# Decoder kernel: the 64-tap causal filter as one 64x64 triangular block for each channel, the two short filters on GpSimd, and new orders of the steps

## The reference, cut to what matters

```
def _dwconv(x, w):                      # x: sequence, token, channel; w: channel, K taps
    K = w.shape[1]
    xt = pad(transpose(x, (0, 2, 1)), K - 1 zeros ahead)
    y = conv(xt, w[:, None, :], groups = channels)     # y[c, t] = sum_s w[c, K-1-s] * v[c, t-s]
    return transpose(y, (0, 2, 1))

v = silu(_dwconv(hs @ Wv, conv_v))
paths = stack([_dwconv(v, fir_s),       # 3 taps
               _dwconv(v, fir_m),       # 15 taps
               _dwconv(v, fir_l),       # 64 taps
               delta_path,              # delta rule, chunks of 32 tokens
               v])
gate_in = concatenate([hs, stats(paths)])          # mean, square, absolute value, norm
probs = softmax((gelu(gate_in @ gW1 + gb1) @ gW2 + gb2) / tau)
o = einsum('blhp,blhpd->blhd', probs, paths)       # then a norm and @ Wo
```

## Time and profile before

| what | value |
|---|---|
| median of 3 runs | 1418.63 us (1417.29 to 1436.04) |
| span of the profiled execution | 1418.5 us |
| PE busy in the span | 1334.8 us, 94% |
| DVE, ACT, POOL busy | 991.1, 682.2, 137.9 us (70%, 48%, 10%) |
| mean granted TensorE clock | 0.975 of full |

### The profile page before, as it was taken

How to read it: one execution, slowest core, us unless ns; L and a number is a source line. 1 busy time by engine, 2 the same in 40 slices (tenths; PEclk the granted TensorE clock), 3 DMA queues, 4 the chain that set the end, 5 groups by cost and what they waited for, 6 DMA issues and landing times.

```text
span 1418.5 us, 42978 instructions
## 1 busy us (share of the span) xinstructions
PE 1334.8 (94%) x18644; PEld 1166.4 (82%) x18644; DVE 991.1 (70%) x2959; ACT 682.2 (48%) x1735; POOL 137.9 (10%) x299
## 2 busy tenths in 40 slices
PE   6999998999986899999999999999999999999997
PEld 6788887888643689899789889788979879989976
DVE  7957898678689554667784567796457778455767
ACT  3535763448377456333447533346632444743332
POOL 3111121111110010100110100011010010010000
PEclk9989999999997899999999999999999999999999
DMA  5000000000230200000000000000000000000001
GB/s 160 2 3 2 3 2 2 3 2 3 77 139 19 77 2 1 2 3 2 2 2 1 2 3 3 1 2 1 1 2 4 2 3 1 1 1 3 3 2 31
DMA packets 8509, 20.33 MB, mean 14 GB/s; under 512 B 2304, under 2 KB 6400, under 8 KB 7808
## 3 DMA queue, kind: packets, MB, share of 16 engines
q1 hardware_dynamic: 8320, 17.58, 3.5%
HBM read 16.53 MB, written 1.05 MB: 12 GB/s over the span
## 4 chain that ended last, share of the span: by engine, by line
PE 47%; DVE 12%; ACT 4%; issue 2%; POOL 1%; DVEq 0%
PE PS L2210 6%; PE PS L2337 6%; PE PS L1935 4%; PE PS L1967 3%; PE PS L1956 3%; PE PS L1922 3%; PE PS L2220 3%; PE PS L589 2%; PE PS L690 2%; ACT AR L1985 2%; PE PS L1947 2%; PE PS L2669 1%; PE PS L2678 1%; PE PS L1819 1%; DVE X L2740 1%
## 5 line engine op out<-in xcount | busy, mean ns | idle before, releaser
L589 PE MATMUL PS<-CC 128*128 128x128 f32 x1024 | 134.9, 279 | 0.0
L589 PEld LDWEIGHTS PS<-CC 128*128 128x128 f32 x1024 | 124.5, 193 | 3.1 <-issue 0.5
L1985 ACT ACTIVATE AR<-PS,SC 128x128 f32<-128x128 f32 x256 | 91.1, 378 | 39.3 <-DVE SC L2013 39.3
L2337 PE MATMUL PS<-AR,PA 64*64 64x256 f32 (+43 forms) x2624 | 108.6, 300 | 0.5 <-issue 0.4
L2210 PEld LDWEIGHTS PS<-AR 64*64 64x64 f32 x3072 | 100.5, 135 | 7.2 <-issue 2.2
L2210 PE MATMUL PS<-AR 64*64 64x32 f32 (+1 forms) x3072 | 103.1, 219 | 0.8 <-DVE AR L2463 0.3
L576 POOL TENSOR_SCALAR SC<-mv 128x2 f32<-128x2 f32 x64 | 13.2, 206 | 837.0 <-DVE mv L562 818.4
L2337 PEld LDWEIGHTS PS<-AR,PA 64*64 64x64 f32 x2624 | 85.0, 133 | 6.9 <-issue 2.7
L2010 DVE TENSOR_REDUCE SC<-PS 128x4 f32<-128x512 f32 x64 | 44.2, 691 | 57.1 <-PE PS L1935 56.7
L1935 PE MATMUL PS<-kvt,AR 128*128 128x128 f32 x512 | 68.8, 279 | 2.6 <-ACT AR L1980 2.6
L1935 PEld LDWEIGHTS PS<-kvt,AR 128*128 128x128 f32 x512 | 63.2, 191 | 7.9 <-ACT AR L1980 6.6
(11 more groups left out here) (552 smaller groups left out, 3334.6 us busy)
## 6 DMA issues: line engine op xcount, KB each, us to landing
WC<-in_cw SPq DMA_DIRECT2D x1, 5438.5 KB, 15.8
PA<-in_fd SPq DMA_DIRECT2D x1, 2624.0 KB, 9.3
PA<-in_stat SPq DMA_DIRECT2D x2, 1280.0 KB, 12.0
X<-in_x SPq DMA_DIRECT2D x2, 512.0 KB, 5.5
out<-X SPq DMA_DIRECT2D x1, 1024.0 KB, 5.3
CC<-in_const SPq DMA_DIRECT2D x1, 809.0 KB, 4.4
PA<-in_aw SPq DMA_DIRECT2D x1, 653.0 KB, 7.4
PA<-in_intw SPq DMA_DIRECT2D x1, 576.0 KB, 5.8
```

Source lines behind the costliest of these rows:

```text
L589: T.matmul(bank[int(b)][:, 0:P], lhsT=ident, rhs=CC[:, 0:P], start=True, stop=True)
L1985: A.activation(d.blocks[:, h, :], d.bank[:, h * P:(h + 1) * P], ACT.Exp, scale=D2 ** -0.5, bias=d.most[:, h:h + 1], accum_out=d.total[:, h ...
L2337: m = T.matmul(out_[:, :, first:SEQ], lhsT=FD[rows, tap:tap + 64], rhs=d.vp[rows, :, first + 1 - shift:SEQ + 1 - shift], start=starts, sto ...
```

## The change

1. `fd` holds, for each channel, the 64x64 triangular matrix of the 64-tap filter (64 columns of 64 by 64: `NFD` falls from 82x64 to 64x64 columns; `PA` keeps its size). Rows are the input tokens, columns the output tokens.
2. `v` must therefore lie with its tokens on the partitions: 8 more matmuls of 64x64 by 64 columns at the transpose of `v`, and one ACT copy of 256 columns (`v_seqs`).
3. The 64-tap filter becomes 64 x 2 matmuls a unit, weights 64x64, and only 4 columns each (the four sequences of the unit). Channel pairs alternate between output halves, so the order still goes through all four quarters.
4. The 3- and 15-tap filters go to POOL as chain 2 and 3 of its order: 18 `tensor_scalar` and 16 `tensor_tensor` of 128 partitions by 4 x (64 - shift) elements a unit, each waiting for the one before on its own engine, in 18 steps.
5. ACT copies 128 columns in place of 512 twice; the laying out is 4 transposes (of the short filters) and 8 matmuls of 64x64 by 64 columns, with a wait of PE on its own first half and a wait on POOL's `short`. ACT has one copy fewer to `paths`, and its `path_squares` waits for POOL's `short` as well, since it writes where `v` lies.
6. All orders of parts A and C are new. `FILL_A` goes from 139 to 87 digits, `FILL_C` from 373 to 524. The streams of part C stand side by side in the old order; in the new one stream 0 goes ahead by about the length of the delta layer.

The diff, without the lists of numbers:

```
-FILTERS = ((3, 0), (15, 3), (64, 18))
-NFD = 82 * 64
+SHORT = ((3, 0), (15, 3))
+NPA, NFD = 82 * 64, 64 * 64
...
-        FILL_A = (139 digits)      FILL_C = (373 digits)
+        FILL_A = (87 digits)       FILL_C = (524 digits)
...
+                self.vs = ar[:, 768:1024].rearrange("p (q n) -> p q n", q=SQ)
...
             for j in range(TS):
-                m = T.transpose(ps[:, 3, j * P:(j + 1) * P], d.s3[:, 512 + j * P:512 + (j + 1) * P], ident)
+                T.transpose(ps[:, 3, j * P:(j + 1) * P], d.s3[:, 512 + j * P:512 + (j + 1) * P], ident)
+            for q in range(SQ):
+                for rows in d.halves:
+                    m = T.matmul(ps[rows, 3, ST + q * SEQ:ST + (q + 1) * SEQ],
+                                 lhsT=d.s3[rows, 512 + q * SEQ:512 + (q + 1) * SEQ], rhs=cc("ident64")[rows, :],
+                                 start=True, stop=True)
...
-            for n, pair in enumerate(taps):
...
+            T.wait_ge(*a.at(f"{k}.v_seqs"))
+            T.wait_ge(*a.at(f"{k}.local"))
+            T.wait_ge(fd_there, 16)
+            for i in range(64):
+                c, o = i % 2, i // 2 * SQ
+                for r, rows in enumerate(d.halves):
+                    m = T.matmul(ps[64 * c:64 * c + 64, r, o:o + SQ], lhsT=FD[rows, i * 64:i * 64 + 64],
+                                 rhs=d.vs[rows, :, i], start=True, stop=True)
+                if (i + 1) * FGROUPS // 64 > i * FGROUPS // 64 and i < 63:
+                    yield
             m.then_inc(*p.up(f"{k}.fir"))
             yield
             T.wait_ge(*a.at(f"{k}.fir1"))
+            laid_out(0).then_inc(*p.up(f"{k}.filtered_even"))
+            T.wait_ge(*st.pool.at(f"{k}.short"))
+            (4 transposes of d.short)
+            T.wait_ge(*p.at(f"{k}.filtered_even"))
+            m = laid_out(1)
             m.then_inc(*p.up(f"{k}.filtered"))
...
+        def pool_l3_attention_aside(st):
+            k, d, g = "L3a", Delta(st), st.pool
+            G.wait_ge(*st.act.at(f"{k}.v"))
+            G.wait_ge(*st.pe.at(f"{k}.grams1"))
+            for f, (K, at) in enumerate(SHORT):
+                for shift in range(K):
+                    ...
+                    if shift:
+                        G.wait_ge(*g.now())
+                    G.tensor_scalar(term if shift else sum_, v_, weight, None, ALU.mult).then_inc(*g.up())
+                    if shift:
+                        G.wait_ge(*g.now())
+                        G.tensor_tensor(sum_, sum_, term, ALU.add).then_inc(...)
+                    yield
...
+            A.activation(d.vs, ps[:, 3, ST:2 * ST].rearrange("p (q n) -> p q n", q=SQ), ACT.Copy, scale=0.5)
...
             A.wait_ge(*v.at(f"{k}.path_delta"))
+            A.wait_ge(*g.at(f"{k}.short"))
             A.square(...)
```

More of the change, by code:

```diff
@@ L2176, in __init__ @@
                 self.gram, self.lt = pairs(3584), pairs(4096)
-                self.fir = [ar[:, o:o + 512] for o in (3584, 4608)]
+                self.fir = [ar[:, o:o + 128] for o in (3584, 4608)]
+                self.short, self.term = st.short, ar[:, 0:ST]
                 self.up = [pairs(4608 + 512 * n) for n in range(5)]
@@ L2194, in __init__ @@
                 self.halves = [slice(64 * b, 64 * b + 64) for b in range(2)]
-        def filter_taps():
-            one = [(0, s) for s in range(3)] + [(2, s) for s in (0, *range(2, 13), *range(13, 64, 2))]
-            two = [(1, s) for s in range(15)] + [(2, s) for s in (1, *range(14, 64, 2))]
-            assert len(one) == len(two) == 41
-            return list(zip(one, two))
+        FGROUPS = 14
         def tensor_l3_attention(st):
@@ new lines, in tensor_l3_attention_aside @@
+            laid_out(0).then_inc(*p.up(f"{k}.filtered_even"))
+            T.wait_ge(*st.pool.at(f"{k}.short"))
+            for j in range(TS):
+                for f in range(2):
+                    o = (2 * j + f) * P
+                    T.transpose(ps[:, 0, o:o + P], d.short[:, f, j * P:(j + 1) * P], ident)
+            T.wait_ge(*p.at(f"{k}.filtered_even"))
+            m = laid_out(1)
+            m.then_inc(*p.up(f"{k}.filtered"))
+            yield
[5 more added lines that the diff above has]
+                for shift in range(K):
+                    weight = wc("L3a_short")[:, at + K - 1 - shift:at + K - shift]
+                    sum_, term = (b.rearrange("p (q t) -> p q t", q=SQ)[:, :, shift:SEQ] for b in (d.short[:, f, :], d.term))
+                    v_ = d.vp[:, :, 1:SEQ + 1 - shift]
+                    if shift:
[3 more added lines that the diff above has]
+                        G.wait_ge(*g.now())
+                        G.tensor_tensor(sum_, sum_, term, ALU.add).then_inc(*g.up(f"{k}.short" if f and shift == K - 1 else None))
+                    if not (f and shift == K - 1):
+                        yield
@@ L2421, in scalar_l3_attention @@
                          scale=0.5).then_inc(*a.up(f"{k}.path_v"))
+            A.activation(d.vs, ps[:, 3, ST:2 * ST].rearrange("p (q n) -> p q n", q=SQ), ACT.Copy, scale=0.5).then_inc(
+                *a.up(f"{k}.v_seqs"))
             yield
@@ L2815, in tensor_aside_c, with pool_aside_c @@
                 yield from tensor_l3_attention_aside(sd)
+        def pool_aside_c(sd):
+            for i in range(NITER):
+                begin(sd, "c", i)
+                yield from pool_l3_attention_aside(sd)
         def next_head(hd, i):
@@ L2989, in decoder @@
                                           ("vector", vector_part_c, vector_aside_c, vector_head_c),
[L2990 removed]
+                                          ("pool", pool_part_c, pool_aside_c, pool_head_c)):
             fill = [tensor_fill(FILL_C)] if engine == "tensor" else []
[L2992 removed]
+            chains = [part(st) for st in streams] + [aside(sd) for sd in asides] + [head(hd) for hd in heads]
             take_turns(chains + fill, TURNS_C[engine])
@@ L3052 @@
     cw["L3a_cw"] = rows(np.stack([a3[f"conv_{n}"].T for n in "qkv"]))
-    fir = np.concatenate([a3["fir_s"], a3["fir_m"], a3["fir_l"]], axis=1)
-    fd = np.zeros((P, fir.shape[1], 64), np.float32)
-    fd[np.arange(P), :, np.arange(P) % 64] = fir
+    cw["L3a_short"] = np.concatenate([a3["fir_s"], a3["fir_m"]], axis=1)
+    fd = np.zeros((P, 64, 64), np.float32)
+    long = a3["fir_l"].reshape(2, 64, 64)
+    for s_ in range(SEQ):
+        for r in range(2):
+            fd[64 * r + s_, :, s_:] = long[r][:, ::-1][:, 0:SEQ - s_]
     path = [0, 1, 2, 4, 3]
```

80 lines of the change are left out of this document (31 added, 49 removed), and 299 rows, old and new, of tables (TURNS_A, TURNS_C).

## The result

The changed kernel takes 1480.92 us in the median of 4 runs (1478.02 to 1481.14), the kernel before 1422.45 us in 4 runs beside it. The ratio is 1.039, 95% interval 1.0339 to 1.0441: slower, where 1387 us had been forecast and 1428 us was the end of the range. The profiled execution took 1478.02 us with a span of 1476.7 us.

A forecast was written before the change was run, and what follows sets the result against it. The prediction took PE, with its fixed order, as the bound: work plus idle time. From 1418.5 us, -41.8 us (-28.3 in part C, -13.5 in A) and +10 us idle gave 1387 us, range 1368 to 1428.

The forecast's parts named there:

- the opening one: Whole kernel: PE's order is fixed, so time is its work plus idle time, 24, 20 and 40 us in A, B, C.
- PE's work removed and added: Part C's filters: 108.6 us removed; 33 us for 2048 new passes, 4.3 for `v_seqs`, 3 for laying out added.
- The rival of a fixed cost a pass: New filter on PE at 33.6 ns a pass: 69 us, 36 more, 1423 us in all; chance 8%.
- The fill: PE's fill matmuls: 151 more in part C, +40.0 us; 52 fewer in part A, -13.5 us.
- The term for part C: Fill in part C: 151 more matmuls at 0.265 us each, +40.0 us.
- the gain of 13.5 us: Part A: 52 fewer fill matmuls at 0.260 us each, counted as 13.5 us less time.
- Idle time: PE in part C: runs of fill go from 80 to 155, leaving gaps open, +10 us; ends nothing and +16 us.
- POOL's new chain: Short filters on POOL: 21.6 us a unit, tensor_scalar at 0.45 us, hidden behind 23 to 27 us of PE's steps.
- the slower rival: POOL becomes the bound: chain 31.6 us a unit, PE waits for `short`, +61 us, 1448 us; chance 10%.
- DVE and POOL: Delta layer: the two engines disturb each other through shared SBUF ports; priced 0 to +25 us, 0 taken.
- The prediction's own sum for part C: Part C: net -28.3 us from filter and fill, +10 us of idle time.
- the filter's term: Filter on PE in part C: old passes' 108.6 us replaced by 33 us, priced at 76 us less.

The follow-up runs named there:

- e3: Kernel before, its filters' tap passes cut to their first 4 columns except those starting a sum: 1499.9 us, ratio 1.054 to the kernel before.
- e1: Changed kernel with the long filter's passes 64 columns wide in place of 4: 1462.2 us, ratio 1.027 to the kernel before.
- e9: Changed kernel with 151 of the 524 fill steps in part C left out: 1481.3 us, ratio 1.040 to the kernel before.
- e2: Changed kernel with only the first product of each short filter left on POOL: 1444.3 us, ratio 1.014 to the kernel before.
- e15: Changed kernel with 32-column long-filter passes and POOL's chain on its own buffer, its sums unread: 1466.9 us, ratio 1.027 to the kernel before.
- e12: Changed kernel with 32-column long-filter passes and only each short filter's first product on POOL: 1411.1 us, ratio 0.989 to the kernel before.
- e8: Changed kernel's order, fill and laying-out, but the old filter's passes in number and width on PE, none on POOL: 1463.0 us, ratio 1.023.
- e11: Changed kernel with the long filter's passes 32 columns wide, POOL's chain kept: 1475.2 us, ratio 1.032 to the kernel before.
- e16: Second run of the changed kernel with 32-column long-filter passes, POOL's chain kept: 1479.4 us, ratio 1.037 to the kernel before.
- e5: Changed kernel with 64-column long-filter passes and only each short filter's first product on POOL: 1435.0 us, ratio 1.005 to the kernel before.
- e4: Kernel before, its filters' tap passes cut to their first 64 columns except those starting a sum: 1421.6 us, ratio 0.995.

## Why the prediction was wrong

**The step that failed** is the opening one, that "a time is the sum of what stands in PE's order plus its idle time", with each pass at the price it has today. That holds at one clock only. The old filter's passes are 256 to 4 columns wide; making all of them 4 wide took PE's clock away in the delta layers, and with it the price of everything there. No part of the text and no rival had the clock in it, though the rows that it used carry the granted clock as a column. In part C's +59.6 us the clock is some +80 to +90 (an estimate from the granted clock, above), and all the rest together -20 to -30. The experiments show it from both sides: e3 (the old kernel with thin passes, 5.4% slower) and e1 (the new one with thick passes, 1.2% faster).

**PE's work removed and added.** 16 ns a pass was nearly right at the full clock: in the best stretch 49 passes start in 0.74 us.

```profile
584.89 0.93 PE L2340 MATMUL PS<-AR,PA 64*64 64x4 f32 x49
585.63 0.24 PE L2216 MATMUL PS<-AR 64*64 64x32 f32 x1
```

Over all of part C it is 20 ns from start to start at the full clock and 34 ns at the lower one, at which 976 of the 2048 passes ran. So the term came out at 61.8 us. The rival of a fixed cost a pass named a time near this, 69 us, for another reason.

**The fill.** The term for part C was counted rightly (1024 passes in these windows against 746, at 164.4 us even more than the +40), but in the changed kernel it decides nothing: without it the time is the same (e9). In part A it was wrong outright. The fill fell from 36.20 to 26.92 us and PE's busy time by 13.4 us:

```profile
0.00:390.00 390.00, 353.03 (x5631) 300.54 (x5632) 308.01 (x955) 197.09 (x447) 69.47 (x144) 0.96 0.07 23
```

But the wide matmuls of L529 that end part A still begin at 379.1 us (L527 before, 379.0); PE is idle 37.0 us in this window where it was 23.6. A fill that covers a wait gives the wait back when it goes. The text had said just that of the filter and did not apply it to the fill: the gain of 13.5 us was counted as time.

**Idle time.** +10 us foreseen, -10.5 us measured in part C. That at half clock PE's own work lasts longer and covers more is a likely reason, not a tested one. (The new list of turns has 156 runs of fill, not 155.)

**POOL's new chain.** The tensor_scalar is the mis-sized term: 0.45 us taken, 0.89 us measured in the median and 0.98 in the mean, so about 32 us a unit. That is the chain of the slower rival (31.6 us, 7.6 over the cover, +61 us). Its size was right and its place wrong. After the change PE doesn't wait for the chain at L2362 at all; in e1 it does, 6.1 us in all. The waits that the chain makes are mostly those for the norms queued behind it, which the prediction had named and not priced: 8 of 12.4 us between e2 and the changed kernel, and in e15, with the readers taken away, 24 of 30. The rest of its cost is busy time of PE, with more of it at the lower clock.

**DVE and POOL.** 0 to +25 us were foreseen and 0 taken; DVE got 21 us of work more (e2). The masks show it: 0.676 us each before, 0.800 after.

```profile
L2497 DVE TENSOR_TENSOR AR<-AR,CC 128x512 f32<-128x512 f32 x40 | 32.0, 800 | 0.8 <-ACT AR L2457 0.8
```

**What was right.** With most of the clock kept and POOL's chain away (e12), part C takes 925.2 us and the kernel is faster, by 1.1% (0.6 to 1.6). The prediction's own sum for part C was 933.8 - 28.3 + 10, about 915 us. But e12 computes next to nothing of the short filters, which that sum had for free on POOL. From e8 to e12, in the same order, the shorter long filter and the dropped short ones give some 50 us, less than the 76 us of the filter's term, at 32 columns a pass and with some clock still missing.

**What stays open.** With 4, 32 and 64 columns POOL's chain costs 0.025, 0.043 to 0.048 and 0.022 in the ratios, about 36, 61 to 69 and 31 us (after less e2, e11 and e16 less e12, e1 less e5). No run explains why it costs most with 32; that PE then has the least work to cover a late norm is an argument, not a finding. The traces add a hint. In e16 seven of the ten falls of the clock in the delta layers begin during an idle time of PE of 1 to 3.4 us or within 1.5 us of its end, and e16 has 127 us of part C at the lower level; in e12, without these waits, it has 50. In the changed kernel, with 4 columns, only two of ten begin so. Whether the waits cause the falls with 32 columns was not tested. Nor was the norms' work taken off POOL's queue while the chain stays, which would settle the share of the queue. No kernel tried that computes all of it beats the one before: on PE, POOL or DVE, in this order, the short filters cost more than the shorter long filter gives.

## What to carry to other kernels

Before making TensorE's passes thinner, ask what the clock will do: look at the granted clock beside the busy time in each stretch, since a full PE line says nothing of it. Widening a pass with columns that nobody reads can be faster than the bare result, up to a point (without POOL's chain 1.014 with 4 columns, 0.989 with 32, 1.005 with 64). A long chain put on a free engine is paid for by what stands behind it in that engine's queue; price those small steps and not only the chain's reader.

## What the runs showed of the hardware

The clock fell to its lower level, 1.2 GHz, with PE busy for every one of the 7 us before and stayed there for 68 us of unbroken work (e3), while the same kernel with passes of up to 64 columns kept the time of the one before (e4: ratio 0.995 against 1.054). At the two levels a 64x64 pass of 32 columns took 31 and 53 ns from start to start, one of 4 columns 20 and 34 ns (the changed kernel). Without POOL's chain, making the passes 32 columns wide in place of 4 took the time at the lower level in part C from 138 to 50 us (e2, e12). One multiplication by a scalar for each channel on POOL, over 200 to 252 columns, took 0.89 us in the median, more than the addition of two tensors of the same size (0.68 us), and 0.81 us with a constant. DVE did multiplication and addition together in 0.46 us. A 128x512 product of two SBUF tensors on DVE took 0.800 us in the mean while POOL's chain ran, 0.676 without it.
